# First norm's statistics from VectorE to ScalarE in an RWKV-6 and mixture-of-experts layer

## The reference

```
xx = x[t-1] - x[t];  m = tanh((x + xx*maa_x) @ w1)          # token shift, four low-rank mixes
xw, xk, xv, xr = x + xx*(maa_w + mw), ...
r = xr @ W_r;  k = xk @ W_k;  v = xv @ W_v                  # 16 heads of 16
w = exp(-exp(decay + tanh(xw @ dw1) @ dw2))
y_t = r_t (S + u k_t v_t);  S = w_t S + k_t v_t             # scan over the tokens of a sequence
y = (y - mean) * rsqrt(var + 1e-5) * ln_g + ln_b            # the "first norm", over 256 channels
x = layernorm(x + y @ W_o)                                  # the second norm
p = softmax(x @ gate_w + gate_b);  top 2 of 32 experts, capacity 1.2 x mean
x = layernorm(x + sum_k p_k * (gelu(x @ w1_e + b1_e) @ w2_e + b2_e))   # the last norm
```

## Time and profile before

| | |
|---|---|
| time of three runs | 2341.23, 2342.44 and 2346.23 us; median 2342.44 |
| profiled execution | 2343.03 us; span in the trace 2341.3 us |
| mean granted clock of TensorE | 0.922 |
| busy over the span | TensorE 1938.1 (83%), its weight loads 1336.8, VectorE 1834.2 (78%), ScalarE 1059.1 (45%), GpSimd 1373.3 (59%) |
| experts, 1400 to 2240 us | TensorE busy for 840 of 840 us, granted clock 1.00 |
| last norm, 2286.9 to 2341.3 us | share of the DMA engines 0.92, 309 GB/s; ScalarE busy for 37.65 us |

### The profile page before, as it was taken

The page is one execution under the profiler, slowest core; times in us unless marked ns, Lnnn a source line. Parts: engine busy times, 40 slices in busy tenths (PEclk is TensorE's granted clock), DMA queues, the critical chain, the costliest instruction groups (busy, mean ns, idle before and its releaser), DMA issues. The chain is left out here.

```text
span 2341.3 us, 33041 instructions
## 1 busy us (share of the span) xinstructions
PE 1938.1 (83%) x9894; PEld 1336.8 (57%) x9894; DVE 1834.2 (78%) x3157; ACT 1059.1 (45%) x1919; POOL 1373.3 (59%) x954
## 2 busy tenths in 40 slices
PE   5777888788777887877776299999999999999980
PEld 2333343333333333433332189999999999999970
DVE  2899999899999998999997266666666666666655
ACT  2233553345334543444432255555555555555546
POOL 3667787768777787678775224444444444454440
PEclk9889999899989998999886599999999999999995
DMA  6932111111112111111020144545454545455538
GB/s 163 220 87 64 46 46 54 47 54 36 51 47 58 29 51 42 58 29 49 31 69 20 58 122 121 122 121 120 120 120 122 120 120 121 120 123 122 124 57 287
DMA packets 172844, 209.00 MB, mean 89 GB/s; under 512 B 12796, under 2 KB 152480, under 8 KB 172768
## 3 DMA queue, kind: packets, MB, share of 16 engines
q1 hardware_dynamic: 112688, 143.09, 20.7%
q0 software_dynamic: 28672, 34.78, 8.6%
q10 hardware_dynamic: 31408, 30.33, 5.0%
HBM read 118.65 MB, written 75.53 MB: 83 GB/s over the span
## 5 line engine op out<-in xcount | busy, mean ns | idle before, releaser
L807 DVE TENSOR_TENSOR_SCAN S<-wT,S,vb 128x512 f32<-128x512 f32 x512 | 624.9, 1262 | 0.0
L1070 POOL TENSOR_TENSOR prod<-S,rT 128x2048 f32<-128x2048 f32 x128 | 536.8, 4198 | 148.0 <-DVE S L807 147.8
L1289 PE MATMUL up<-x_parts,w_parts 128*128 128x308 f32 x3072 | 464.2, 307 | 1.5 <-DVE x_parts L1402 1.5
L1304 PE MATMUL down<-w_parts,h_parts 128*128 128x512 f32 (+1 forms) x1280 | 452.4, 396 | 0.0
L1289 PEld LDWEIGHTS up<-x_parts,w_parts 128*128 128x128 f32 x3072 | 439.2, 189 | 4.1 <-issue 1.8
L1364 POOL TENSOR_TENSOR ye<-ye,weight 128x256 f32<-128x256 f32 (+1 forms) x160 | 197.7, 1235 | 379.9 <-DVE ye L1458 379.9
L1342 ACT ACTIVATE h_full<-up,b_now 128x616 f32<-128x616 f32 x256 | 198.6, 776 | 421.2 <-PE up L1289 409.6
L1372 POOL DMA_INDIRECT sums<-ye,sum_at x160 | 281.6, 1760 | 150.1 <-POOL ye L1364 140.0
L1445 DVE TENSOR_TENSOR h_parts<-h_full,h_parts 128x616 fp32r<-128x616 f32 x256 | 206.8, 808 | 193.1 <-ACT h_parts L1342 192.8
L1307 PE MATMUL down<-w_parts,h_parts 128*128 128x256 f32 (+1 forms) x1280 | 357.4, 279 | 0.0
L571 PE MATMUL vb<-v_stack,pick_v 128*128 128x512 f32 x512 | 216.7, 507 | 152.0 <-DVE S L807 151.8
(11 more groups left out here) (176 smaller groups left out, 2645.2 us busy)
## 6 DMA issues: line engine op xcount, KB each, us to landing
w_raw<-in_L_ffn_w_dram SPq DMA_DIRECT2D x64, 1024.0 KB, 8.8
expert_in_rows<-y_tok ACTq DMA_DIRECT2D x30, 652.5 KB, 9.1
xe<-expert_in_rows SPq DMA_DIRECT2D x32, 522.0 KB
v_stack<-v_parts SPq DMA_DIRECT2D x64, 256.0 KB, 4.5
x_tok<-in_L_attn_x_dram SPq DMA_DIRECT2D x16, 512.0 KB, 3.3
x_res<-in_L_attn_x_dram SPq DMA_DIRECT2D x16, 512.0 KB, 3.4
sums<-x_row SPq DMA_DIRECT2D x16, 512.0 KB, 2.9
rows<-sums SPq DMA_DIRECT2D x16, 512.0 KB, 5.5
```

The source lines that it names most:

```text
L807: dve.tensor_tensor_scan(line[:, 1:TC + 1], wT[:, par, half, :], vb[:, p % 2, g, :], line[:, 0:1], ALU.mult, ALU.add).then_inc(scanned, 1)
L1070: pool.tensor_tensor(prod[:, q % 2], S[:, q % RING, :, 0:TC], rT[:, par, half, None, :].to_broadcast([P, QUAD, TC]), ALU.mult).then_inc(pr ...
L1289: last = pe.matmul(up[:, f % 2, half, 0:HC], w1_parts[:, par, wp, k, f * P:(f + 1) * P], x_parts[:, par, xp, k, half * HC:(half + 1) * HC] ...
L1304: pe.matmul(down[0:m, (par * TILES + t) % 2, :, :], h_parts[:, 0, f, t * P:t * P + m], w2_parts[:, par, :, f, :], start=f == 0, stop=False)
```

## The change

The statistics of the first norm no longer use bn_stats. ScalarE drains the turned y in four instructions of 128x256 instead of two of 128x512, and each leaves the sum of its rows (`accum_out`) in `total`. In slot 8, which now is `stat1`, ScalarE makes the negated mean from the sums and squares the deviations, four instructions with the negated mean as bias; their row sums go to `square`, the squares themselves to a scratch tile. In slot 10 the root is taken of square/C + eps. Reciprocal, offsets and normalization stay. The second norm keeps its bn_stats. Besides, `rows_of` in `last_norm` gives a partition four neighbouring rows, for load and store, where it gave rows 128 apart.

```diff
@@ -186,8 +186,11 @@
         y_tok = sb("y_tok", [P, TPC, C])
         x_res = sb("x_res", [P, TPC, C])
         x1_row = sb("x1_row", [P, TPC, C + FIELDS])
-        stats = sb("stats", [P, 2, TPC, 6])
-        mv = sb("mv", [P, 2, TPC, 2])
+        stats = sb("stats", [P, TPC, 6])
+        mv = sb("mv", [P, TPC, 2])
+        total = sb("total", [P, TPC])
+        square = sb("square", [P, TPC])
+        squares = sb("squares", [P, TPC, C])
         rstd = sb("rstd", [P, 2, TPC])
         offset = sb("offset", [P, 2, TPC])
         minus_mean = sb("minus_mean", [P, 2, TPC])
@@ -259,6 +262,7 @@
         res_loaded = sem("res_loaded")
         x1_stored = sem("x1_stored")
         s_dve = sem("s_dve")
+        squared = sem("squared")
         root_done = sem("root_done")
         normed = sem("normed")
         tanh_done = sem("tanh_done")
@@ -320,12 +324,12 @@
         NSHORT = len(DVE_MIXES) * NH
         XM_OF = {"w": 0, "k": 1, "v": 2, "r": 0}
-        C_AT = {"turn": 6, "stat1": 9, "root1": 10, "norm1": 12, "back": 14, "wo0": 17, "z0": 18, "wo1": 19,
+        C_AT = {"turn": 6, "stat1": 8, "root1": 10, "norm1": 12, "back": 14, "wo0": 17, "z0": 18, "wo1": 19,
                 "z1": 20, "stat2": 21, "root2": 22, "norm2": 23, "x1T": 25, "gate": 27, "top": 28, "ratio": 28,
                 "count": 30, "place": 30, "scatter": 31}
         NCF = 10
-        LN1_AT = 2 * TPC + 1
+        LN1_AT = 1
         X1_AT = LN1_AT + 2 * TPC + 1
         GAP_AT = X1_AT + 2 * TPC + 1
         HITS_AT = GAP_AT + 4
@@ -716,18 +720,7 @@
                 dve.wait_ge(root_done, stage_value(i, 2, which + 1))
                 dve.reciprocal(rstd[:, which, :], rstd[:, which, :]).then_inc(s_dve, 1)
-            def statistics(src, which):
-                for t in range(TPC):
-                    dve.bn_stats(stats[:, which, t, :], src[:, t, :]).then_inc(s_dve, 1)
-
             def stage_c(i, par, s):
-                if s == C_AT["stat1"]:
-                    dve.wait_ge(c_drained, stage_value(i, NCF, 2))
-                    statistics(y_tok, 0)
-                    chain(i, TPC)
-                    dve.sem_inc(wait_carrier, 1)
-                    for t in range(TPC):
-                        dve.bn_aggr(mv[:, 0, t, :], stats[:, 0, t, :]).then_inc(s_dve, 1)
                 if s == C_AT["norm1"]:
                     invert(i, 0)
                 for k in range(2):
@@ -742,11 +735,12 @@
                                           x_res[:, 2 * k:2 * k + 2, :], ALU.add).then_inc(c_drained, 1)
                 if s == C_AT["stat2"]:
                     dve.wait_ge(c_drained, stage_value(i, NCF, 6))
-                    statistics(x1, 1)
+                    for t in range(TPC):
+                        dve.bn_stats(stats[:, t, :], x1[:, t, :]).then_inc(s_dve, 1)
                     chain(i, LN1_AT + TPC)
                     dve.sem_inc(wait_carrier, 1)
                     for t in range(TPC):
-                        dve.bn_aggr(mv[:, 1, t, :], stats[:, 1, t, :]).then_inc(s_dve, 1)
+                        dve.bn_aggr(mv[:, t, :], stats[:, t, :]).then_inc(s_dve, 1)
                 if s == C_AT["norm2"]:
                     invert(i, 1)
                 if s == C_AT["top"]:
@@ -907,8 +901,10 @@
                         if isinstance(i, int) and i == 0:
                             act.wait_ge(s_fill, 16 * FILLS)
-                        act.activation(y_tok[:, 2 * k:2 * k + 2, :], pc[:].rearrange("p (t c) -> p t c", t=2),
-                                       ACT.Copy).then_inc(c_drained, 1)
+                        for t in range(2):
+                            ins = act.activation(y_tok[:, 2 * k + t, :], pc[:, t * C:(t + 1) * C], ACT.Copy,
+                                                 accum_out=total[:, 2 * k + t:2 * k + t + 1])
+                        ins.then_inc(c_drained, 1)
                     if s == C_AT["back"] + k:
                         act.wait_ge(c_full, stage_value(i, NCF, 3 + k))
                         for h in range(NH):
@@ -919,13 +915,22 @@
                         act.wait_ge(c_full, stage_value(i, NCF, 7 + k))
                         act.activation(yT[:, :, 2 * k * P:(2 * k + 2) * P], pc[:].rearrange("p (h t) -> p h t", h=NH),
                                        ACT.Copy).then_inc(c_drained, 1)
-                for which, name in enumerate(("root1", "root2")):
-                    if s == C_AT[name]:
-                        act.wait_ge(s_dve, stage_value(i, NCH, (2 * TPC, LN1_AT + 2 * TPC)[which]))
-                        act.activation(rstd[:, which, :], mv[:, which, :, 1], ACT.Sqrt, bias=eps_col[:, 0:1]
-                                       ).then_inc(root_done, 1)
-                        act.activation(minus_mean[:, which, :], mv[:, which, :, 0], ACT.Copy, scale=-1.0
-                                       ).then_inc(mean_kept, 1)
+                if s == C_AT["stat1"]:
+                    act.wait_ge(c_drained, stage_value(i, NCF, 2))
+                    act.activation(minus_mean[:, 0, :], total[:], ACT.Copy, scale=-1.0 / C).then_inc(mean_kept, 1)
+                    act.wait_ge(mean_kept, stage_value(i, 2, 1))
+                    for t in range(TPC):
+                        ins = act.activation(squares[:, t, :], y_tok[:, t, :], ACT.Square,
+                                             bias=minus_mean[:, 0, t:t + 1], accum_out=square[:, t:t + 1])
+                    ins.then_inc(squared, 1)
+                if s == C_AT["root1"]:
+                    act.wait_ge(squared, stage_value(i, 1, 1))
+                    act.activation(rstd[:, 0, :], square[:], ACT.Sqrt, bias=eps_col[:, 0:1], scale=1.0 / C
+                                   ).then_inc(root_done, 1)
+                if s == C_AT["root2"]:
+                    act.wait_ge(s_dve, stage_value(i, NCH, LN1_AT + 2 * TPC))
+                    act.activation(rstd[:, 1, :], mv[:, :, 1], ACT.Sqrt, bias=eps_col[:, 0:1]).then_inc(root_done, 1)
+                    act.activation(minus_mean[:, 1, :], mv[:, :, 0], ACT.Copy, scale=-1.0).then_inc(mean_kept, 1)
                 for which, (name, rows, ready) in enumerate((("norm1", y_tok, LN1_AT), ("norm2", x1, X1_AT))):
                     if s == C_AT[name]:
                         act.wait_ge(s_dve, stage_value(i, NCH, ready))
@@ -1505,7 +1510,7 @@
         normed = sem("normed")
         def rows_of(dram, first, g):
-            return dram[bass.ds(g * (GT * P) + first, GT * P), :].rearrange("(t p) c -> p t c", p=P)
+            return dram[bass.ds(g * (GT * P) + first, GT * P), :].rearrange("(p t) c -> p t c", t=GT)
         def groups(eng, body):
 
```

## The result

| | before | changed | ratio (95% interval) |
|---|---|---|---|
| median of 8 runs each | 2342.21 us | 2330.69 us (2322.02 to 2333.27) | 0.995 (0.9934 to 0.9965) |
| profiled execution, and its span | 2343.03, 2341.3 | 2332.65, 2330.9 | |

The kernel is faster by 11.5 us. The forecast, 2326, was 4.7 too low, and the time lies inside the range. Cut at the same events, the two traces differ as follows; "scans" goes from the token shift of chunk 1 (line 683) to the end of the last scan, "tail" from there to the end of the last scatter.

A forecast was written before the change was run, and what follows sets the result against it. VectorE, 92% busy in the scans, was taken to set the pace on average. Bodies 17.6, plus clock 2.0, minus tail 3.3, plus last norm 0.5, gave 16.8 us off 2343.0: 2326 us, 8 in 10 between 2315 and 2338.

The forecast's parts named there:

- VectorE's stretch of 1.84: In body 7, the 1.84 us from the removed statistics to VectorE's next multiply, expected to be freed.
- two kinds by K0's releaser: Bodies 1 to 14: in eight K0 waits for VectorE's scan, in six for GpSimd's k mix.
- Rival 1: VectorE keeps all 1.84 us in each of the 15 bodies: 26.8 us gained, 2316 us; chance 10 in 100.
- rival 2: GpSimd's late scatters set the pace in every body: 3.2 us gained, 2340 us; chance 11 in 100.
- rival 4: ScalarE's row sums cost more than a whole pass, over 0.5 us each: about 2345 us; chance 2 in 100.
- body 15: The body that prepares no chunk; its offsets wait for VectorE's reciprocal, so all moves: 1.8 us gained.
- the six bodies from which I had 11.0: Bodies 1, 5, 7, 9, 11, 13, where K0 moves with VectorE's scan: 1.84 us each, 11.0 gained.
- bodies 6 and 12: Bodies counted with VectorE's scan, but with GpSimd's k mix ending later: 1.2 us each, 2.4 gained.
- the six behind GpSimd: Bodies 2, 3, 4, 8, 10, 14, where K0 starts right behind GpSimd's mix: 0.4 us each, 2.4 gained.
- rival 3: TensorE falls to 1.2 GHz in front of v, slow K0 costing 1.7 us per body: 2354 us; chance 5 in 100.
- the slow K0: K0 at half clock in five of eight bodies, some 6.7 us too long; 2.0 taken as gained, bounds 0 to 6.7.
- the tail: For chunk 15 nothing covers ScalarE's drains, Squares, sums and table load: 3.3 us lost, bounds 2.5 and 4.7.

The follow-up runs named there:

- no statistics: Changed kernel with no first-norm statistics on any engine (mean taken as 0, variance as 1, no row sums or Squares): 2328.27 us.
- both engines: Changed kernel with VectorE's bn_stats and bn_aggr of the first norm back in, results unused: 2344.24 us.
- Squares twice: Changed kernel with the four Squares and their row sums made twice in every chunk: 2330.47 us.
- put-off scatters: Four of GpSimd's eight scatters per chunk moved behind the next body's k and v mixes: 2344.11 us on the kernel before, 2327.89 on the changed one.
- the two kernels that add fillings: Changed kernel, four scatters moved later, unread TensorE products in the tail: 2331.04 us; with fewer of these, and some before R0 in every body: 2309.42 us.
- the filler ahead of R0: Changed kernel, four scatters moved later, 7 and 5 unread tail products, one and a half unread products before R0 in every body: 2309.42 us.
- the early table: Changed kernel with one Sqrt of a single column ahead of the tail's first drain, to load the square-root table early: 2330.89 us.

## Why the prediction was right, and where it was off

**Right.** VectorE's stretch of 1.84 went, the spread's wait fell from 2.55 to 0.74 (forecast 0.7), and the bodies from 1 to 14 divide in two kinds by K0's releaser. In those that GpSimd sets VectorE gives time back around v: 0.34 and 0.53 in body 8. ScalarE's part is hidden in the bodies; no statistics, both engines and Squares twice show it from three sides. By the rows a sum adds 0.09, where I took 0.1. Rival 1 (VectorE keeps everything) falls by the new waits, rival 2 (GpSimd everywhere, 3 us gained) by the six bodies in which K0 moved with the scan, rival 4 by the 0.09.

**Off: what comes of the 1.84 in each body.** The scans gave 15.6 where I had 19.6; averaged over four profiles with VectorE's statistics and six without (scatters in place, the doubled Squares left out; the four take in the put-off scatters, which left the scans as they were) it is 1206.4 - 1193.5 = 12.9. VectorE's busy time fell by 24.4 in these, and its idle time rose by 11.6: above all at v from 2.9 to 8.9, at 52 to 64 us from 6.0 to 10.5, and in front of the w mix from 12.0 to 13.5. Cut by bodies (from one token shift to the next, body 15 from its first scan to its last), these averages give 9.7 for the six bodies from which I had 11.0, 0.6 for bodies 6 and 12 (forecast 2.4), 1.7 for the six behind GpSimd (2.4), 0.1 for body 15 (1.8) and 0.7 for body 0 (nothing). Three steps failed.

- *The count of bodies.* I gave GpSimd six and counted bodies 6 and 12 among the eight, at 1.2 each. They joined the six: the k mix decides as soon as VectorE's scan comes 1.84 earlier, since GpSimd's products and scatters take as long as before (4.20 and 0.99 us each on both pages). The put-off scatters show the cause: the waits at v fall to 0.
- *Body 15.* I let all of its 1.84 through, since it prepares no chunk. It took 64.54 us from its first scan to its last where it was 64.59. TensorE and VectorE there, first in the kernel before, then in the changed one:

```profile
1230.24 1.94 PE L581 MATMUL ypsum<-prod,sum_y 128*32 128x512 f32 x8 [4.60 <-POOL prod L1070]
...
1233.25 1.26 DVE L800 TENSOR_TENSOR vb<-vb,kT 128x512 f32<-128x512 f32 x2
```

```profile
1215.85 1.94 PE L585 MATMUL ypsum<-prod,sum_y 128*32 128x512 f32 x8 [4.34 <-POOL prod L1075]
1217.72 2.08 PE L575 MATMUL vb<-v_stack,pick_v 128*128 128x512 f32 x4
1218.55 1.30 DVE L794 TENSOR_TENSOR vb<-vb,kT 128x512 f32<-128x512 f32 x2 [1.43 <-PE vb L575]
```

GpSimd starts its first product behind the eight scatters, 14.6 us after the body's first scan in both kernels; TensorE's sums wait for it, and the next spread stands behind the sums. VectorE, now early, gives back 1.43. That wait is 1.43 to 1.45 in all seven profiles without VectorE's statistics and with the scatters in place, and none of the four with the statistics has it. With the scatters put off alone it is gone, and the body took 62.14. (In the two kernels that add fillings it is gone too, but there VectorE waits for W_o and the gate, and the body took 65.5 and 65.7.)
- *The next meeting point.* In the bodies I followed the saving to v and no further. At R0 the body meets GpSimd again (the r mix), and TensorE's clock. This is rival 3's mechanism at another place. K0 ran slow (over 2.5 us) in five to seven bodies with VectorE's statistics and in none or one without (three with the doubled Squares), so the slow K0 that I had bounded by 6.7 went almost wholly, where I took 2.0 of it. But R0 was slow in 3 to 6 bodies before and in 8 or 9 after. The two all but exclude each other: over the thirteen profiles without the filler ahead of R0, R0 was slow in 2 of the 28 bodies in which K0 was, and in 94 of the 154 others. So with K0 at full clock the slow product is more often R0: bodies with either one slow were 8 to 13 before and 8 or 9 after. Filling the wait removed it, and the scans became 13 us shorter. Why the low clock comes to one of the two and seldom to both no run here tells.

**Off by size: the tail.** I had 3.3 up to the root. It is 2.1. A drain grew by 0.23 per half, not by 0.42 and two sums: two pieces with their sums take 0.83, less than the 1.02 of the nearest row. And the four Squares with their sums take 2.09, what the norm's four take without any. The other 1.9, nearly all of it W_o's second product at half clock, I hadn't seen: no term of the tail had TensorE's clock. It came in five profiles with a wait of 8.2 us or a longer one ahead of the transposes and in none of the four with 6.3 or less; but with put-off scatters alone it was 2.00 after 8.17, and with the early table 3.78 after 6.89, so the length of the wait alone doesn't settle it. The two errors cancel to +0.7, which is luck.

The Trainium skill (ScalarE: Activation LUTs, What ACT_TABLE_LOAD costs) counts a drain of some 1.4 us with each switch. The tail shows none: 0.01 ahead of a load of 1.28 and 0.02 behind it, so the table load costs what I took from the earlier trace rows.

**The last norm** gained 1.0 to 1.3 in every kernel with the new row order, twice what I took and at the upper bound of 1.2. The experts took 948.5 to 950.2 us in all kernels, with the same instructions, on average 0.9 longer in the ten profiles without VectorE's statistics than in the four with them; why, I can't say.

## What to carry to other kernels

When work leaves a pacing engine, follow the saving from one meeting point to the next through the whole period: each one that another engine sets takes a part of it, and where one is removed (the scatters) the next (R0) can take the waits over. A body in which the engine prepares nothing has such points too (body 15). A wait of 1.5 to 2 us in front of a product on the critical way, as here at R0, is worth a look at the granted clock behind it, over all periods, and not in one; filling it with products that nobody reads gave as much here (scans 13 us shorter) as the change itself. A filler has to be sized by a measured row, or it costs what it should save.

## What I had not expected of the hardware

With the same code and the same wait of 1.47 us in front of it, R0 ran at 2.4 GHz in some bodies of an execution and at 1.2 in others; behind waits of 0.4 to 0.9 us it never ran slow in the kernel with the filler, and K0 behind a spread that waited 0.73 in none of the bodies of the changed kernel. The Trainium skill (TensorE: Matmul & The Clock Gate, A second HAM failure mode: psum-queue depth-cycling) describes, for a kernel that cycles through PSUM banks, a clock that swings between its two levels where TensorE pauses briefly and often; R0's rows agree on the two levels, with 0.50 and 1.00 behind the same wait, and the bank cycling no run here tests. The clock is also the likeliest cause of the 10 us between runs of one kernel: with the put-off scatters the mean granted clock was 0.933 in the run of 2316.99 us and 0.925 in that of 2334.41. That is a correlation; no run separates it from other causes.
